# Softmax sums and head outputs by DMA instead of TensorE in a decoder layer with cross attention

## What is computed

```python
x = _layernorm(x + _L0_attn_ref(x, ...), axis=-1)
x = _layernorm(x + _L0_xattn_ref(x, ctx_1024, mask, ...), axis=-1)
x = _layernorm(x + _L0_ffn_ref(x, ...), axis=-1)

# cross-attention: q, k, v split into 16 heads of 16
scores = jnp.einsum('bhqd,bhkd->bhqk', q, k) / jnp.sqrt(16.0)
attn = jax.nn.softmax(jnp.where(mem_mask, scores, -jnp.inf), axis=-1)
out = jnp.einsum('bhqk,bhkd->bhqd', attn, v)
return out.transpose(0, 2, 1, 3).reshape(B, LQ, H * Dh) @ Wo.T
```

## Time and profile before

| | |
|---|---|
| median of 3 runs | 1702.16 us (1699.74 to 1702.57) |
| the profiled execution, its own time | 1697.87 us |
| its span (first to last instruction) | 1696.1 us |
| PE busy | 1619.5 us, 95% |
| DVE busy | 1235.1 us, 73% |
| ACT busy | 1062.5 us, 63% |
| POOL busy | 161.5 us, 10% |
| DMA | 116.58 MB, mean 69 GB/s |

### The profile page before, as it was taken

The page is one execution under the profiler, slowest core; times in us unless marked ns, Lnnn a source line. Parts: engine busy times, 40 slices in busy tenths (PEclk is TensorE's granted clock), DMA queues, the critical chain, the costliest instruction groups (busy, mean ns, idle before and its releaser), DMA issues.

```text
span 1696.1 us, 25766 instructions
## 1 busy us (share of the span) xinstructions
PE 1619.5 (95%) x9848; PEld 607.4 (36%) x9848; DVE 1235.1 (73%) x1790; ACT 1062.5 (63%) x2012; POOL 161.5 (10%) x151
## 2 busy tenths in 40 slices
PE   6779999999999999999999999999999999999987
PEld 5442323432333334333334334333334333332234
DVE  6787777877778777877778767877778777776423
ACT  2227676766666666676666766676666766666651
POOL 7311000100010000100010000100001000000000
PEclk9889999999999999999999999999999999999999
DMA  5673170706135160715317070623407050420000
GB/s 154 118 161 71 34 137 5 127 25 121 43 68 91 54 105 12 128 37 104 60 42 109 21 134 24 102 63 81 82 9 131 25 86 26 83 31 2 4 25 16
DMA packets 101342, 116.58 MB, mean 69 GB/s; under 512 B 21834, under 2 KB 86987, under 8 KB 101220
## 3 DMA queue, kind: packets, MB, share of 16 engines
q1 hardware_dynamic: 98484, 113.89, 34.1%
q10 hardware_dynamic: 2736, 1.06, 0.3%
...
## 4 chain that ended last, share of the span: by engine, by line
PE 83%; DVE 6%; ACT 5%; issue 5%; DMA 1%; POOL 1%; ACTq 0%; SPq 0%; POOLq 0%; DVEq 0%
PE banks L1107 22%; PE values L1126 22%; PE banks L1081 11%; PE work L990 5%; PE work L1004 5%; ACT xprobs L1263 4%; PE work L947 4%; PE work L1011 3%; PE work L1017 3%; PE work L932 3%; DVE xneg_max_pieces L1451 2%; PE work L1020 1%; PE work L996 1%; PE work L1029 1%; DVE xv_rows L1409 1%
## 5 line engine op out<-in xcount | busy, mean ns | idle before, releaser
L1263 ACT ACTIVATE xprobs<-banks 128x512 f32<-128x512 f32 x1664 | 902.4, 595 | 440.5 <-PE banks L1107 425.6
L1451 DVE TENSOR_REDUCE xneg_max_pieces<-banks 128x2 f32<-128x1024 f32 x768 | 910.0, 1220 | 273.2 <-PE banks L1081 271.1
L1107 PE MATMUL banks<-xq_stacks,xk_stacks 99*128 99x512 bf16 (+1 forms) x1664 | 523.3, 385 | 16.2 <-ACT xprobs L1263 8.5
L1126 PE MATMUL values<-xprobs,xv_rows 128*17 128x512 f32 x3328 | 437.9, 598 | 1.0 <-ACT xprobs L1263 1.0
L1107 PEld LDWEIGHTS banks<-xq_stacks,xk_stacks 99*128 99x128 bf16 (+1 forms) x1664 | 128.9, 97 | 412.3 <-ACT xprobs L1263 281.3
L1081 PE MATMUL banks<-xk_stacks,xq_stacks 49*128 49x512 bf16 (+1 forms) x2048 | 249.7, 335 | 10.7 <-DVE xneg_max_pieces L1451 9.0
L1081 PEld LDWEIGHTS banks<-xk_stacks,xq_stacks 49*128 49x128 bf16 x2048 | 56.8, 94 | 273.7 <-DVE xneg_max_pieces L1451 156.0
L1518 POOL TENSOR_TENSOR xk_parts<-xk_rest,xk_parts 128x401 bf16<-128x401 f32 (+1 forms) x64 | 59.0, 921 | 705.4 <-ACT xk_parts L1224 705.4
L1126 PEld LDWEIGHTS values<-xprobs,xv_rows 128*17 128x17 f32 x3328 | 55.1, 95 | 120.4 <-issue 118.9
L1513 POOL TENSOR_TENSOR xrstd<-xrstd,mhalf 128x4 f32<-128x4 f32 x23 | 23.2, 1010 | 647.5 <-DVE xrstd L1323 647.5
L1004 PE MATMUL work<-xvT,ctxT_a 128*128 128x128 f32 (+1 forms) x416 | 57.2, 282 | 3.1 <-DVE xk_rest L1384 2.0
...
## 6 DMA issues: line engine op xcount, KB each, us to landing
xk_stacks<-key_parts_dram SPq DMA_DIRECT2D x186, 200.1 KB, 11.8
...
xq_stacks<-parts_dram SPq DMA_DIRECT2D x186, 64.0 KB, 8.1
...
```

Source lines behind the costliest of these rows:

```text
L1107: pe.matmul(scores[n % SRING], kst[0:ROWS[par], k, h2, par, t * P:(t + 1) * P], qst[0:ROWS[par], k, h2, par, :], start=True, stop=True).th ...
L1126: last = pe.matmul(av[32 * j:32 * j + HD + 1, :], vals[:, k, t, gr * GH + j, :], probs[:, sl % 2, j, :], start=t == 0, stop=t == XKT - 1)
L1263: nc.scalar.activation(probs[:, sl % 2, j, :], scores[n % SRING], ACT.Exp).then_inc(exped, 1)
L1451: nc.vector.tensor_reduce(nmp[:, of % 2, j2, :, q, piece], pairs[n % MRING][:, :, :], AX.X, ALU.max, negate=True).then_inc(on["mxr"], 1)
```

## The change

The `otr`, `oT` and `max` shorts go. After ACT's copy of `av`, SP moves the softmax sums of the four heads into `xrsum` (128 x 16) and the outputs, in four DMAs of 16 x 512, to their feature rows in `oT` (`xo_by_dims`). DVE inverts `xrsum`. The inverses are written to DRAM (`rsum_dram`) and read back, each head's row spread over 16 partitions, and DVE multiplies (`scale`). For groups 0 and 2 of a batch SP does the write and the spread; for groups 1 and 3 ACT does them, at the ends of the third and fourth slot of the next group. The maxima are turned by DVE itself (32 x 32 blocks), and SP writes and reads them. `v 1` stands ahead of `xo` now and `x2T 0` at slot 14. In the last group the scores use six banks and stand together ahead of the values, and the tail turns only the last group's outputs.

```diff
-            1: ("otr", 3, PREV), 2: ("oT", 0, PREV), 4: ("oT", 1, PREV), 8: ("x1T", 0, NEXT), 10: ("max", 1, NOW),
-            11: ("x1T", 1, NEXT), 12: ("x2T", 0, PREV), 14: ("otr", 0, NOW), 16: ("x2T", 1, PREV), 18: ("v", 3, NOW),
-            23: ("max", 2, NOW), 27: ("otr", 1, NOW), 35: ("loss", 0, PREV), 36: ("max", 3, NOW),
-            41: ("otr", 2, NOW), 49: ("max", 0, NEXT),
+            8: ("x1T", 0, NEXT), 11: ("x1T", 1, NEXT), 14: ("x2T", 0, PREV), 16: ("x2T", 1, PREV), 18: ("v", 3, NOW),
+            35: ("loss", 0, PREV),
...
-            (("kproj", 0, NEXT), 1), (("kproj", 1, NEXT), 1), (("v", 0, NOW), 2), (("xo", 0, PREV), 2),
-            (("xo", 1, PREV), 2), (("v", 1, NOW), 2), (("kproj", 2, NEXT), 1), (("kproj", 3, NEXT), 1),
+            (("kproj", 0, NEXT), 1), (("kproj", 1, NEXT), 1), (("v", 0, NOW), 2), (("v", 1, NOW), 2),
+            (("xo", 0, PREV), 2), (("xo", 1, PREV), 2), (("kproj", 2, NEXT), 1), (("kproj", 3, NEXT), 1),
...
+            1: [("invert", "o", 3, PREV)], 4: [("aggr", "x1", 0, NEXT)],
+            14: [("invert", "o", 0, NOW)], 18: [("scale", "o", 0, NOW)],
+            27: [("invert", "o", 1, NOW)], 32: [("scale", "o", 1, NOW)],
+            40: [("invert", "o", 2, NOW)], 44: [("scale", "o", 2, NOW)],
             2: norm_steps("stats", "x1", 0, 2, NEXT), 3: norm_steps("stats", "x1", 2, 4, NEXT),
-            4: [("aggr", "x1", 0, NEXT)], 5: norm_steps("apply", "x1", 0, 2, NEXT),
-            6: norm_steps("apply", "x1", 2, 4, NEXT), 7: norm_steps("stats", "x2", 0, 2, PREV),
-            8: norm_steps("stats", "x2", 2, 4, PREV), 9: [("aggr", "x2", 0, PREV)],
-            10: norm_steps("apply", "x2", 0, 2, PREV), 11: norm_steps("apply", "x2", 2, 4, PREV),
+            5: [*norm_steps("apply", "x1", 0, 2, NEXT), ("scale", "o", 3, PREV)],
+            6: norm_steps("apply", "x1", 2, 4, NEXT), 8: norm_steps("stats", "x2", 0, 2, PREV),
+            9: norm_steps("stats", "x2", 2, 4, PREV), 10: [("aggr", "x2", 0, PREV)],
+            11: norm_steps("apply", "x2", 0, 2, PREV), 12: norm_steps("apply", "x2", 2, 4, PREV),
...
-                    pe.wait_ge(on["w_free"], ph.order.after(("oT", 1, b)))
-                last = rows_of(W, x2T, xoT, i, units(part, parts, 2 * CH))
+                    pe.wait_ge(scaled, GROUPS * (b + 1))
+                last = rows_of(W, oT, xoT, i, units(part, parts, 2 * CH))
...
+        def score_bank(n):
+
+            if n < LAST_SCORE:
+                return scores[n % SRING], SRING
+            place = n - LAST_SCORE
+            before = SRING if place < SRING else LAST_RING if place >= LAST_RING else n + 1
+            return g.banks[:, place % LAST_RING, :], before
...
+            final = m == B * GROUPS - 1
+            for j in range(GH if final else GH // 2):
+                pe_scores(m, t, j)
...
-            pe_scores(m, t, 3)
+            if not final:
+                pe_scores(m, t, 2)
+                pe_scores(m, t, 3)
```

ACT, DVE and SP:

```diff
-                nc.scalar.wait_ge(on["w_full"], MAIN.order.after(("otr", i, b)))
+                nc.scalar.wait_ge(moved, N_MOVED * m)
...
+        def act_inverses_out(m):
+
+            nc.scalar.wait_ge(inverted, m + 1)
+            nc.scalar.wait_ge(spread, 16 * (m - 1)) if m >= 2 else None
+            nc.scalar.dma_start(g.rsum_dram[m % 2].rearrange("j (s x) -> (j s) x", x=GH * T // P),
+                                rs[:, m % 2, :]).then_inc(rs_out, 16)
+
+        def act_spread_inverses(m):
+
+            nc.scalar.wait_ge(rs_out, 16 * (m + 1))
+            if m >= 2:
+                nc.scalar.wait_ge(scaled, m - 1)
+            nc.scalar.dma_start(rsb[half_rows(m)[1], :],
+                                g.rsum_dram[m % 2].unsqueeze(1).broadcast_to([GH, HD, T])).then_inc(spread, 16)
...
+            if m and m % NG == 0:
+                if t == 2:
+                    act_inverses_out(m - 1)
+                if t == 3:
+                    act_spread_inverses(m - 1)
...
+            elif name == "invert":
+                m = GROUPS * b + q
+                v.wait_ge(moved, N_MOVED * (m + 1))
+                v.reciprocal(rs[:, m % 2, :], rs[:, m % 2, :]).then_inc(inverted, 1)
+            elif name == "scale":
+                m = GROUPS * b + q
+                k, half = divmod(q, NG)
+                these = slice(half * P // 2, (half + 1) * P // 2)
+                v.wait_ge(spread, 16 * (m + 1))
+                v.tensor_tensor(oT[these, k, :], oT[these, k, :], rsb[these, :], ALU.mult).then_inc(scaled, 1)
...
+                dve_mark(v.tensor_copy(comb[:, :, 0, :], by_parity))
             elif step == 2:
                 dve_settle()
-                v.tensor_tensor(comb[:, 1, :], nm[:], comb[:, 0, :], ALU.subtract).then_inc(on["comb_ready"], 1)
+                dve_mark(v.tensor_tensor(comb[:, :, 1, :], by_parity, comb[:, :, 0, :], ALU.subtract))
+            else:
+                if of >= 2:
+                    v.wait_ge(on["mrow_out"], 16 * (of - 1))
+                elif of == 1:
+                    v.wait_ge(front["mrow_out"], 16)
+                dve_settle()
+                v.transpose(mrow[:], comb[:].rearrange("p e r n -> p (e r n)")).then_inc(on["comb_ready"], 1)
...
+            sp.dma_start(g.max_dram.rearrange("r (b c) -> b r c", c=32), mrow[:]).then_inc(on["mrow_out"], 16)
+            sp.wait_ge(on["mrow_out"], 16 * n)
...
+                sp.dma_start(qst[row:row + 2, k, gr * GH // 2:(gr + 1) * GH // 2, par, :],
+                             src[par]).then_inc(on["max_in"], 16)
...
+            sp = nc.sync
+            k, half = divmod(m % GROUPS, NG)
+            sp.wait_ge(evac, m + 1)
+            if m >= GROUPS:
+                sp.wait_ge(on["w_full"], MAIN.order.after(("xo", 1, m // GROUPS - 1)))
+            sp.dma_start(rs[:, m % 2, :], oS[HD::2 * HD, :].rearrange("j (s x) -> j s x", x=GH * T // P)).then_inc(moved, 16)
+            for j in range(GH):
+                row = half * P // 2 + j * HD
+                sp.dma_start(oT[row:row + HD, k, :], oS[2 * HD * j:2 * HD * j + HD, :]).then_inc(moved, 16)
+
+        def sp_spread_inverses(m):
+
+            sp = nc.sync
+            k, these = half_rows(m)
+            sp.wait_ge(inverted, m + 1)
+            if m >= 2:
+                sp.wait_ge(spread, 16 * (m - 1))
+            sp.dma_start(g.rsum_dram[m % 2].rearrange("j (s x) -> (j s) x", x=GH * T // P), rs[:, m % 2, :]).then_inc(rs_out, 16)
+            sp.wait_ge(rs_out, 16 * (m + 1))
+            if m >= 2:
+                sp.wait_ge(scaled, m - 1)
+            sp.dma_start(rsb[these, :], g.rsum_dram[m % 2].unsqueeze(1).broadcast_to([GH, HD, T])).then_inc(spread, 16)
```

SP's order in a batch, and the tail of PE:

```diff
                 sp_load_x(1)
             if prev >= 0:
+                sp_move_outputs(m - 1)
                 sp_load_x1(prev)
             sp_stacks(b, 1)
             if nxt < B:
-                use = 2 * NP * b
                 if b:
                     sp_free_key_dram(nxt, 0)
                 sp_key_parts(0, use)
                 sp_key_parts(1, use + 1)
                 sp_store_x1(nxt)
+            sp_max_rows(m + 1)
+            if nxt < B:
                 sp_key_parts(2, use + 2)
                 sp_key_parts(3, use + 3)
+            sp_move_outputs(m)
+            if nxt < B:
                 sp_query_parts(0, uses_before(0, nxt))
+            sp_spread_inverses(m)
+            sp_max_rows(m + 2)
+            if nxt < B:
                 sp_free_key_dram(nxt, 1)
                 sp_key_parts(4, use + 4)
                 if nxt + 1 < B:
                     sp_load_ctx(nxt + 1)
+            sp_move_outputs(m + 1)
+            if nxt < B:
                 sp_stacks(nxt, 0)
                 if nxt + 1 < B:
                     sp_load_x(nxt + 1)
                 sp_key_parts(5, use + 5)
+            sp_max_rows(m + 3)
+            if nxt < B:
                 sp_key_parts(6, use + 6)
                 sp_key_parts(7, use + 7)
             if prev >= 0:
                 sp_adapter(prev, adp_in)
+            sp_move_outputs(m + 2)
+            sp_spread_inverses(m + 2)
+            if nxt < B:
+                sp_max_rows(m + 4)
+            if prev >= 0:
                 sp_store_out(prev)
             if nxt < B:
                 sp_query_parts(1, uses_before(1, nxt))
...
+
+            def xo(c, first, last):
+                for q in range(first, last):
+                    one = pe.matmul(tail_xo[q], oT[:, c, q * P:(q + 1) * P], xoT[:, c, :], start=c == 0, stop=c == CH - 1)
+                return one
+
+            pe.wait_ge(scaled, B * GROUPS - 1)
+            xo(0, 0, 2)
             pe.wait_ge(evac, B * GROUPS)
             transposes(g.W[:], oS[:].rearrange("p (q n) -> p q n", q=QT), 0).then_inc(t_otr_made, 1)
+            xo(0, 2, QT)
             pe.wait_ge(t_ox_in, 1)
-            for c in range(CH):
-                transposes(tail_w[c], ox, c).then_inc(t_oT_made, 1)
-            for one in t_oT_in:
+            for q in range(QT):
```

(26 more changed lines are left out.)

131 lines of the change are left out of this document (52 added, 79 removed).

## The result

The changed kernel takes 1736.78 us (median of 4 runs, 1729.94 to 1744.35) against 1701.23 before: a ratio of 1.021, interval 1.0164 to 1.0257. It is slower by 35.6 us where 41 us less were forecast, and 1736.78 lies outside the range. The profiled execution took 1739.58 us (span 1737.8, 41.7 more than before).

What follows compares the result with a forecast made beforehand. PE was taken as the bound, with DVE near; 40.8 us from the main loop plus 8.7 from last group, tail and front, less 8 for DVE, gave 41.5 us, hence 1661 us, range 1649 to 1684 (own range 1650 to 1670).

Steps and rivals of the forecast that it cites:

- The waits of ACT: ACT's store, awaited a slot later, lands in 3 to 5 us, up to 4.6 free: cost 0, bounds 0 and 7.2 a time.
- Rival 2: ACT waits for its store, ends of slots 3 and 29; slower from 7.4 us landing: 1714 to 1769, chance 0.08; partly, 0.07.
- what would show it: Signs in the changed profile: plain slots still 3.41 us, slots 1, 2, 4 shorter by 0.6, no DVE scaling wait for the spread.
- 45 shorts of four transposes and `x2T` at slot 12: Main loop, PE: 45 removed shorts at 0.6 us save 27.0 us; moving `x2T 0` from slot 12 saves 4.5 us.
- maxima: Main loop, PE: 31 removed transposes of the maxima at 0.3 us each, bounds 0.23 and 0.42, save 9.3 us.
- last group: Six banks let ACT run without waiting in seven slots without an end job: 4.2 us saved, bounds 0 and 8.
- tail: After the last values product, fewer products and transposes and smaller copies save 2.5 us, bounds 1 and 4.
- front: SP instead of ACT stores and loads the maxima, so PE gets W sooner: 2 us saved, bounds 0 and 4.
- DVE: Crowded slots 5 and 9 make PE wait: 1.1 us a batch, 8 in all, bounds 0 and 20 (2.9 a batch).
- rival 3: Removed transposes weren't the bound; only waits and ends gain, half of 36 us stays: 1679, chance 0.05.
- rival 1: DVE becomes the bound in a batch's first 14 slots: 20 us instead of 8, about 1673, up to 1678, chance 0.18.
- SP's waits ahead of the stacks: SP's moves start the 26 stack DMAs up to 5 us later; stacks and maxima still arrive in time: cost nothing.

Runs made afterwards that it cites:

- experiment 2: Changed kernel, but SP issues the 26 stack transfers of slot 0 only when group 3's spread has landed: 1683.99 us, ratio 0.9911 to the kernel before.
- experiment 5: Changed kernel with half the bytes in the stack transfers of slot 0, as many transfers, made for time alone: 1654.47 us, ratio 0.9718 to the kernel before.
- experiment 6: Changed kernel with group 3's store and spread issued by GpSimd's queue instead of ACT's: 1733.45 us, ratio 1.0186 to the kernel before.
- experiment 4: Changed kernel with 24 idle products on PE in slot 6, ahead of the wait for the scaled outputs: 1743.81 us, ratio 1.0232 to the kernel before.
- experiment 3: Changed kernel with group 3's store and spread issued by SP ahead of the stacks: 1654.85 us, ratio 0.9724 to the kernel before.
- experiment 8: Kernel before with only the last group's scores over six banks, four products of a slot together: 1693.98 us, ratio 0.9953.

## Why the prediction was wrong

**The step that failed** is "The waits of ACT": "a transfer of another queue isn't behind that", so a landing of 3 to 5 us, cost 0. The store of group 3 landed in 7.0 us in batch 2 and up to 8.1. The reading behind it was the earlier trace rows: the share of an instruction fetch rose from 3.0% to 5.5% among stacks. That share counts the time in which a packet is being moved. It can't show the time for which a transfer stands before its first packet moves, and that is what grew: nothing of the spread moved for 7 us. The right rows were there: the earlier trace rows, 8.1 and 11.8 us for the stacks' own transfers, put aside as "behind their own queue". Experiments 2, 5 and 6 show that neither ACT's queue nor GpSimd's gets past the stacks, and that the bytes in front decide.

The prediction drew support from the Trainium skill's page "DMA: Bandwidth & Descriptors", section "Queues, rings and completion order", which says that each engine takes the queues in turn, packet by packet. The passing that the prediction took from this didn't come: 712 packets of SP's queue moved against none of ACT's. No run shows whether ACT's transfer already stood at the engines in that time, which is what the rule speaks of.

**A second omission made it larger.** Rival 2 was the right rival, and had its place at the end of slots 3 and 29. It priced only ACT's wait. The second transfer, the spread, was named only in the part on what would show it ("DVE's scaling shows no wait"), without a price. It leaves after the late store, is itself late behind the same stacks (13.7 us), and PE's `xo` needs it: 57.6 us in slot 6 against 19.2 in slot 4. The price of ACT's wait was near: a landing of 7.0 us is 2.4 over the free 4.6, 17 us in seven batches against the 19.2. At that landing the rival's own threshold of 7.4 us would have left a gain; the second transfer made it a loss. And slot 29 cost nothing in this execution: all six of ACT's waits were in slot 4. In experiment 4 group 1's store was late as well, and slots 30 and 31 cost 22 us more. Of the delays of group 1's spread 6.7 us are paid in slot 34, where DVE stands in its scaling; no product of PE needs the scaled outputs of group 1 before the next batch.

**The clock** was in no part. Behind PE's waits of 4.4 to 8.4 us in slot 6 its products ran at the lower level. From the start of the scaling to V8 the changed kernel takes 53.0 us in seven batches and experiment 3, where PE hardly waits, 40.1: so about 13 of the 82.8 us are the clock there, and the 2.5 us of slot 5 are a further part. Experiment 4 got 11.3 of them back by keeping PE busy.

**The rest of the sum, read from experiment 3**, where the two transfers are out of the way. By slot lengths against the kernel before:

| step | predicted | measured |
|---|---|---|
| 45 shorts of four transposes and `x2T` at slot 12 (slots 1, 2, 4, 12, 14, 27, 41) | 27.0 + 4.5 | 31.8 |
| maxima (slots 10, 23, 36, 49) | 9.3 | 8.3 |
| slot 51, where ACT issued two loads of the maxima | 0 | 3.6 |
| last group (V39 to the last values product) | 4.2 | 6.6 |
| tail | 2.5 | 2.0 |
| front | 2 | 0.1, too small to be told |
| DVE (slots 6 and 11) | -8 | -5.4 |
| slot 34, group 1's spread | 0 | -3.7 |

Together 43.3, where the two spans differ by 43.2; the sum forecast was 41.5, and the 1654.85 us of experiment 3 lie in the forecaster's own range of 1650 to 1670. That the sum came so near is in part luck: several terms are off by 1 to 3.7 us, in both directions, and cancel. The last group's slots without a job took 1.96 us, below the 2.2 forecast, since four exponentials in a row take 1.98 (9.90 us for 20 in experiment 8) and not 2.22. The overrun of 2.9 us a batch in DVE's upper bound is 2.7 by its own rows, which changes nothing. PE was the bound, slot by slot, as the earlier trace rows said; rival 3 is wrong, and rival 1 too: PE waits for DVE's scaling in slot 6 and for its subtraction of a key piece in slot 11, which costs 0.5 and 0.3 us a batch. The price of 0.3 us for the maxima was right only as a mean of 0.49 (slots 10 and 49) and less than 0.1 (slots 23 and 36). SP's waits ahead of the stacks cost nothing in experiment 3, and 26.6 us when they grew by 6 us in experiment 2: the margin that the prediction saw for the stacks was there, but not for the maxima behind them.
